# The last normalization moved to VectorE, its logits made row by row; one-hot matrices ahead of the expert tables; slot weights in two halves

## The chip, the cores and the metric

The kernel runs on one core of a Trainium2 chip. The metric is the device time of one execution in microseconds. A core has TensorE (PE: matrix products and transposes, results in PSUM), VectorE (DVE), ScalarE (ACT), GpSimd (POOL) and SyncE (SP, here the queue that issues most DMAs). Each engine runs its own list of instructions in order; they meet through semaphores, which an instruction raises when it ends and on which another waits.

## What is computed

Two blocks over x (4 batches of 512 rows of 512 values) and a context (4, 512, 256). First a selective state-space block, gated by the normalized x, then a mixture of eight experts in which each row goes to two.

```
x = x + ssm(ctx, z=layernorm(x))          # in_proj, causal conv of 4, silu, x_proj, dt_proj, softplus,
                                          # state = state*exp(d*A) + d*u*B ; y = state.C ; y = (y + D*u)*silu(z)
h = layernorm(x)                          # per row of 512 values, eps 1e-5
logits = h @ gate                         # (rows, 8)
w, idx = top_k(logits, 2); w = softmax(w)
x = x + sum_k w_k * (silu(h @ w0[idx_k]) * (h @ w1[idx_k])) @ wo[idx_k]
```

All matrices are fp32. In the experts each operand is split into two parts (hi and lo) and a product is made of three matmuls.

## The kernel before

**State-space block** (`mamba_block`). Work goes by units: batch (4), half of the channels (2), state (16), so 128 units. In a unit ScalarE makes dA, POOL the input term, VectorE two scans and most of the products with C, POOL the rest; TensorE broadcasts C into the PSUM bank `Cb` (line 663) and adds the unit's transposed states into `yT` (line 682). At the end of a half VectorE gates: g = yT * zsT (`drain_y`, line 572), and POOL adds g to xall (`add_y`, line 298). After a batch's second half come its statistics (`stats_2`, lines 584 and 588, VectorE), a first value of 1/sqrt(var + eps) as exp(-0.5 ln) (`guess_2`, lines 418 to 422, ScalarE), one Newton step and the negated mean (`rstd`, lines 236 to 246, POOL), the normalized rows xlnb (`xln`, line 439, ScalarE, one activation per tile of 128 rows), their transposes (`gate_T`, line 730, TensorE, with copies by ScalarE at line 339), the logits (`logits_of`, line 740, TensorE, all four tiles at once, after the last copies) and their copy (line 577, VectorE). SP stores xlnb and xall (`store_xln`, lines 200 and 201). For batches 0 to 2 all this is woven into the next batch's units; for the last it stands alone at the end. The transposes and logits share two PSUM banks, `pp`, whose uses are numbered in the list `USES`. All engines meet at the end of the block, and SP first waits there for both stores (line 224).

**Expert block** (`ffn_block`). SP loads the first expert's weights in six chunks of 1 MB (line 963). VectorE finds each row's two experts and weights (lines 1180 to 1204); two small matmuls (lines 1399 and 1400) count rows ahead; VectorE turns the counts into a slot for each row (lines 1211 to 1245): `quo` is the slot's tile of 128, `rem` its place there. Then, in this order:
- the tables of experts per tile (lines 1249 to 1275), ending in `tables_ok`, on which SP (line 966, a second load of the first chunks that is made only if the first expert is not number 0, then the next expert's loads, line 976) and ScalarE (the splits `w_hi`, line 1104) wait
- the one-hot matrices: S (line 1279, from quo), S times the row number (line 1284), R (line 1288, from rem, one half per choice k)
- TensorE: 32 matmuls of R and S_tok give the row number of each slot (line 1406)
- VectorE: the split `w_lo` of chunk 0 (line 1294), the token table (lines 1299 to 1305), the split of chunk 1, the weights times S (lines 1360 to 1365), which end in `RS_ok`
- POOL: the index (line 1034) and the gather of 128 rows of xln_dram (line 1040)
- TensorE: `x_T(0, 0)`, four transposes of the gathered rows (line 1415), 32 matmuls of R and S_w that give each slot's weight (line 1470), then `inner(0)`: four products of 12 matmuls (lines 1421 to 1423), each for one chunk. It waits for `xT_lo` (line 1318), and each product for its chunk's `w_lo`.

The loop over tiles follows, with weights changed when the expert does. The slot weights are read (`wtab`, lines 1374 and 1376) after the first tile's step.

## Time and profile before

| | us |
|---|---|
| median of 3 runs | 1330.68 |
| lowest and highest | 1323.72, 1347.05 |
| the profiled execution, its time | 1325.02 |
| its span | 1322.3 |
| mean granted clock of TensorE, as a share of full speed | 0.867 |

Busy share of the span by the profile: TensorE 85%, VectorE 57%, POOL 48%, ScalarE 40%. The profile's times count from the start of its span; the execution's own time is 2.7 us above the span. In the profile PE is TensorE's matmuls, PEld its weight loads, which overlap them. A row of the timeline has start, duration, engine, line, operation, output and inputs with shapes, the number of like instructions merged into it, and in brackets how long the engine had been idle before it and what released it. An fp32 matmul of the state-space block is recorded as two, an fp32 transpose as one.

### The profile page before, as it was taken

How to read it: one execution, taken by the hardware profiler on the slowest of the kernel's cores; microseconds unless marked ns; L12 is line 12 of the kernel's file. 1: busy time of each engine (PE TensorE's matmuls, PEld its weight loads, DVE VectorE, ACT ScalarE, POOL GpSimd, SP SyncE). 2: the span in 40 equal slices, each digit the busy share in tenths (PEclk: the TensorE clock that was granted, in tenths of full speed). 3: DMA queues.
4: the chain of work that ended last, by engine and by line, in shares of the span. 5: the costliest groups of instructions: out<-in, count | busy, mean ns of one | idle time of the engine just before them, and what ended most of it. 6: DMA issues, size and time to landing. Idle time of an engine off the chain costs nothing.

```text
span 1322.3 us, 19385 instructions
## 1 busy us (share of the span) xinstructions
PE 1124.1 (85%) x4940; PEld 837.2 (63%) x4940; DVE 751.0 (57%) x815; ACT 526.0 (40%) x707; POOL 639.7 (48%) x472
## 2 busy tenths in 40 slices
PE   4667988788868877833999999999999999999994
PEld 2234555446444645533788888888888888888883
DVE  3789899887998699837324353442532534324321
ACT  3775655674667464322213232321321323213210
POOL 0399899898989799613023222321222322213221
PEclk8587777686878577855999999999999999999998
DMA  5333232522242224045314243242421524314310
GB/s 180 123 102 103 67 119 88 167 78 91 75 158 82 88 75 156 1 145 204 137 48 167 97 152 125 87 154 76 171 96 48 174 104 160 104 46 174 103 40 25
DMA packets 65445, 145.08 MB, mean 110 GB/s; under 512 B 8655, under 2 KB 11215, under 8 KB 65409
## 3 DMA queue, kind: packets, MB, share of 16 engines
q1 hardware_dynamic: 56368, 116.34, 25.9%
q0 software_dynamic: 9040, 28.32, 6.5%
q8 instruction: 16, 0.26, 0.1%
q14 instruction: 21, 0.16, 0.0%
HBM read 320.53 MB, written 18.35 MB: 256 GB/s over the span
## 4 chain that ended last, share of the span: by engine, by line
PE 52%; DVE 2%; DMA 1%; issue 0%; POOL 0%; ACT 0%; POOLq 0%; DVEq 0%
PE hp L1423 11%; PE hp L1422 10%; PE hp L1421 10%; PE yp L1421 5%; PE yp L1423 5%; PE yp L1422 5%; PE tp L1462 2%; PE xp L1415 1%; PE hp L1406 1%; PE yp L1470 1%; DMA work<-xln_dram,index 0%; DMA work<-out_dram,acc_index 0%; DMA out_dram<-work,out_index 0%; DVE R L1288 0%; POOL index L1034 0%
## 5 line engine op out<-in xcount | busy, mean ns | idle before, releaser
L266 POOL TENSOR_TENSOR ring<-du,bB 128x1024 f32<-128x1024 f32 x128 | 299.3, 2357 | 75.5 <-DVE du L610 52.4
L539 DVE TENSOR_TENSOR_SCAN ring<-dA,ring 128x512 f32<-128x512 f32 x256 | 295.7, 1202 | 17.7 <-ACT dA L349 11.1
L349 ACT ACTIVATE dA<-delta,Acol 128x512 f32<-128x512 f32 x256 | 172.3, 687 | 170.4 <-DVE ring L539 168.0
L1421 PE MATMUL hp<-w_hi,xT_hi 128*128 128x512 f32 x592 | 236.4, 399 | 0.9 <-DVE xT_lo L1318 0.9
L1423 PE MATMUL hp<-w_hi,xT_lo 128*128 128x512 f32 x592 | 236.3, 399 | 0.0
L1422 PE MATMUL hp<-w_lo,xT_hi 128*128 128x512 f32 x592 | 234.1, 395 | 0.0
L682 PEld LDWEIGHTS yT<-ident,ring 128*128 128x128 f32 x1024 | 146.7, 172 | 97.3 <-issue 76.9
L663 PE MATMUL Cb<-xdbl,ident 48*128 48x512 f32 x176 | 126.9, 808 | 87.9 <-DVE ring L545 87.8
L682 PE MATMUL yT<-ident,ring 128*128 128x128 f32 x1024 | 172.9, 332 | 10.7 <-POOL ring L275 10.7
L1339 DVE TENSOR_TENSOR work<-hp,work 128x512 f32<-128x512 f32 x74 | 51.1, 690 | 229.3 <-PE hp L1423 226.2
L1058 POOL COPY out_index<-out_tab 128x1 uint32 x37 | 6.7, 181 | 355.0 <-DVE work L1325 355.0
L1294 DVE TENSOR_TENSOR w_lo<-stage,w_hi 128x2048 fp32r<-128x2048 f32 x48 | 109.1, 2288 | 36.0 <-ACT w_hi L1104 36.0
L1422 PEld LDWEIGHTS hp<-w_lo,xT_hi 128*128 128x128 f32 x592 | 111.6, 189 | 27.0
L1421 PEld LDWEIGHTS hp<-w_hi,xT_hi 128*128 128x128 f32 x592 | 111.8, 189 | 26.3 <-issue 1.1
L1423 PEld LDWEIGHTS hp<-w_hi,xT_lo 128*128 128x128 f32 x592 | 111.4, 188 | 26.1
L1421 PE MATMUL yp<-w_hi,iT_hi 128*128 128x512 f32 x296 | 121.2, 409 | 2.1 <-DVE iT_lo L1350 2.1
L545 DVE TENSOR_TENSOR ring<-Cb,ring 128x1024 f32<-128x1024 f32 x88 | 106.2, 1207 | 25.5 <-PE Cb L663 25.0
L1143 ACT CAST iT_hi<-tp 128x512 fp32r<-128x512 f32 x74 | 39.8, 590 | 194.8 <-PE tp L1462 194.8
L1423 PE MATMUL yp<-w_hi,iT_lo 128*128 128x512 f32 x296 | 116.7, 394 | 0.0
L1422 PE MATMUL yp<-w_lo,iT_hi 128*128 128x512 f32 x296 | 116.2, 393 | 0.0
L1325 DVE SCALAR_TENSOR_TENSOR work<-yp,wtab,work 128x512 f32<-128x512 f32 x37 | 27.8, 751 | 144.1 <-PE yp L1423 137.1
L663 PEld LDWEIGHTS Cb<-xdbl,ident 48*128 48x128 f32 x176 | 32.4, 229 | 119.4 <-DVE ring L545 60.7
(180 smaller groups left out, 1408.6 us busy)
## 6 DMA issues: line engine op xcount, KB each, us to landing
stage<-in_L_ffn_w_kernel_dram SPq DMA_DIRECT2D x160, 1024.0 KB
stage<-in_L_ffn_wo_kernel_dram SPq DMA_DIRECT2D x78, 1024.0 KB
bB<-bcs SPq DMA_DIRECT2D x64, 512.0 KB, 3.6
bC<-bcs SPq DMA_DIRECT2D x40, 256.0 KB, 4.4
xall<-in_x_dram SPq DMA_DIRECT2D x1, 4096.0 KB, 14.8
xln_dram<-xlnb SPq DMA_DIRECT2D x4, 1024.0 KB, 6.9
out_dram<-xall SPq DMA_DIRECT2D x4, 1024.0 KB, 9.1
ctx_rows<-in_ctx_dram SPq DMA_DIRECT2D x4, 512.0 KB, 5.5
```

Source lines behind the costliest of these rows:

```text
L266: g_.tensor_tensor(ring[:, q % RING, :].rearrange("p (e l) -> p e l", e=2), dub(b, h * 2 * L, 2 * L).rearrange("p (e l) -> p e l", e=2), B ...
L349: a_.activation(dA[r % SB][:, :], db(b, eb * L, L), ACT.Exp, scale=Acol[:, eb, n:n + 1]).then_inc(exp_done, 1)
L539: v_.tensor_tensor_scan(o, dA[r % SB][:, :], o, 0.0, ALU.mult, ALU.add).then_inc(scan_done, 1)
L545: v_.tensor_tensor(states, Cb[:, :].unsqueeze(1).to_broadcast([P, 2, L]), states, ALU.mult).then_inc(hc_dve, 1)
L663: t_.matmul(Cb[:, :], ident[0:rows, at:at + 1].to_broadcast([rows, P]), xdbl[:, b % 2, :], start=True, stop=True).then_inc(C_full, 1)
L682: last = t_.matmul(yT[:, t, e * P:(e + 1) * P], ring[:, q % RING, e * L + t * P:e * L + (t + 1) * P], ident[:, :], start=False, stop=(n == ...
L1143: s_.copy(iT_hi[:, 4 * h:4 * h + 4, :], tp[h][:, :].rearrange("p (k t) -> p k t", t=P)).then_inc(i_hi, 1)
L1294: v.tensor_tensor(w_lo[c][:, :, :], stage[c][:, :, :], w_hi[c][:, :, :].bitcast(fp32), ALU.subtract).then_inc(lo_done, 1)
L1339: v.tensor_tensor(inter[:, h, :], hp[2 + h][:, :], gated[:, h, :], ALU.mult).then_inc(inter_done, 1)
L1421: t_.matmul(bank[:, :], a_hi[:, k, :], b_hi[:, b, :], start=(start and k == ks[0]), stop=False)
L1422: t_.matmul(bank[:, :], a_hi[:, k, :], b_lo[:, b, :], start=False, stop=False)
L1423: last = t_.matmul(bank[:, :], a_lo[:, k, :], b_hi[:, b, :], start=False, stop=(stop and k == ks[-1]))
```

## The change

- The last batch's add of g (`add_y` on POOL) becomes a VectorE operation. POOL's `add_y` and `rstd_2` for the last batch go.
- The last batch's first value: VectorE adds eps (`var_last`), ScalarE, told ahead to load a named set of activation tables, does Ln and Exp.
- The Newton step and the negated mean: four VectorE operations in place of six of POOL.
- The copies of transposed tiles 1 and 3 go to VectorE; ScalarE keeps 0 and 2. TensorE makes the logits of a tile (`logits_row`) as soon as the next tile's transposes are issued, in `Cb` and not in a bank of `pp`; before that it waits for all of VectorE's products with C.
- In the routing the one-hot matrices S, S_tok and R come before the expert tables. Both follow on `routed` 31.
- The splits of chunks 0 and 1 on VectorE come after the weights times S.
- The 32 slot-weight matmuls are cut in two: the first sixteen before `x_T(0, 0)`, the others after `inner(0)`. `x_T(0, 0)` itself so comes after a wait for `RS_ok`.

```diff
--- before.py
+++ after.py
@@ -95,6 +95,8 @@
         consts_ok, stats1, rstd1_guess, rstd1_ok = sem("consts_ok"), sem("stats1"), sem("rstd1_guess"), sem("rstd1_ok")
         tap_done, u_ready, bcs_out = sem("tap_done"), sem("u_ready"), sem("bcs_out")
         x1_out = sem("x1_out")
+        logits_out = sem("logits_out")
+        var_last, last_step, logits_last = sem("var_last"), sem("last_step"), sem("logits_last")
         conv_step = [sem(f"conv_step{i}") for i in range(2)]
         abs_done, relu_done, soft_y, soft_w, soft_ln, soft_loss, soft_sub, delta_ready, du_ready, zs_ready = (
             sem(n) for n in ("abs_done", "relu_done", "soft_y", "soft_w", "soft_ln", "soft_loss", "soft_sub",
@@ -117,7 +119,7 @@
             USES += [f"{n}.{b - 1}" for n in ("G0", "G1") if rest]
             USES += [f"{n}.{b + 1}" for n in ("XP", "DT0", "DT1", "DT2", "DT3") if nxt]
             USES += [f"{n}.{b - 1}" for n in ("G2", "G3", "LG") if rest]
-        USES += [f"{n}.{NB - 1}" for n in ("G0", "G1", "G2", "G3", "LG")]
+        USES += [f"{n}.{NB - 1}" for n in ("G0", "G1", "G2", "G3")]
         USE = {n: i for i, n in enumerate(USES)}
 
         def bank(k):
@@ -326,8 +328,6 @@
                         add_ln(b + 1, 0)
                     if s == 31 and b + 1 < NB:
                         times_u(b + 1, 0)
-            add_y(NB - 1, 1)
-            rstd_2(NB - 1)
 
         @block.scalar
         def _(act):
@@ -521,9 +521,13 @@
                     if s == 31 and rest:
                         gate_T(b - 1, 2)
                         gate_T(b - 1, 3)
-            guess_2(NB - 1)
+            a_.preload_act_table_set("natural_log_exp_and_others")
+            act.wait_ge(var_last, 1)
+            a_.activation(rs2[:, 1, :], rs2[:, 0, :], ACT.Ln).then_inc(act_step, 1)
+            act.wait_ge(act_step, 2 * NB + 2)
+            a_.activation(rs2[:, 1, :], rs2[:, 1, :], ACT.Exp, scale=-0.5).then_inc(guess2, 1)
             xln(NB - 1)
-            for i in range(LB):
+            for i in (0, 2):
                 gate_T(NB - 1, i)
 
         @block.vector
@@ -638,8 +642,30 @@
                 times_c(NU - 1)
             logit_copy(NB - 2)
             drain_y(NB - 1, 1)
-            stats_2(NB - 1)
-            logit_copy(NB - 1)
+            b = NB - 1
+            xs = xall[:, b * LB:(b + 1) * LB, 2 * P:4 * P]
+            dve.wait_ge(y_gated, 2 * b + 2)
+            v_.tensor_tensor(xs, g[:, :, :], xs, ALU.add).then_inc(x_added, 1)
+            stats_2(b)
+            dve.wait_ge(stats2, NB)
+            v_.tensor_scalar(rs2[:, 0, :], mv2[:, :, 1], EPS, None, ALU.add).then_inc(var_last, 1)
+            dve.wait_ge(guess2, NB)
+            v_.tensor_tensor(rs2[:, 2, :], rs2[:, 0, :], rs2[:, 1, :], ALU.mult).then_inc(last_step, 1)
+            dve.wait_ge(last_step, 1)
+            v_.scalar_tensor_tensor(rs2[:, 2, :], rs2[:, 2, :], -0.5, rs2[:, 1, :], ALU.mult, ALU.mult).then_inc(last_step, 1)
+            dve.wait_ge(last_step, 2)
+            v_.scalar_tensor_tensor(rs2[:, 3, :], rs2[:, 2, :], 1.5, rs2[:, 1, :], ALU.add, ALU.mult).then_inc(last_step, 1)
+            dve.wait_ge(last_step, 3)
+            v_.scalar_tensor_tensor(nm2[:, :], mv2[:, :, 0], -1.0, rs2[:, 3, :], ALU.mult, ALU.mult).then_inc(rstd2_ok, 1)
+            for i in (1, 3):
+                k = USE[f"G{i}.{b}"]
+                if i == 1:
+                    j = USE[f"LG.{b - 1}"]
+                    dve.wait_ge(filled[j % 2], nth(j))
+                dve.wait_ge(filled[k % 2], nth(k))
+                v_.tensor_copy(gT[:, i, :], bank(k)[:, :]).then_inc(freed[k % 2], 1)
+            dve.wait_ge(logits_last, LB)
+            v_.tensor_copy(logits[:, b * LB:(b + 1) * LB, :].rearrange("p t e -> p (t e)"), Cb[:, 0:LB * 8]).then_inc(logits_out, 1)
 
         @block.tensor
         def _(pe):
@@ -739,6 +765,13 @@
                     for d in range(DI // P):
                         last = t_.matmul(o[:, i * 8:(i + 1) * 8], gT[:, i, d * P:(d + 1) * P], gate[:, d, :], start=(d == 0), stop=(d == DI // P - 1))
                 last.then_inc(done, 1)
+
+            def logits_row(i):
+                k = USE[f"G{i}.{NB - 1}"]
+                pe.wait_ge(freed[k % 2], nth(k))
+                for d in range(DI // P):
+                    last = t_.matmul(Cb[:, i * 8:(i + 1) * 8], gT[:, i, d * P:(d + 1) * P], gate[:, d, :], start=(d == 0), stop=(d == DI // P - 1))
+                last.then_inc(logits_last, 1)
 
             pe.wait_ge(ident_ok, 2)
             pe.wait_ge(small_in, 16 * 9)
@@ -802,9 +835,12 @@
                         logits_of(b - 1)
             for q in range(NU - LAG, NU):
                 acc(q)
+            pe.wait_ge(hc_dve, len(ON_DVE))
             for i in range(LB):
                 gate_T(NB - 1, i)
-            logits_of(NB - 1)
+                if i > 0:
+                    logits_row(i - 1)
+            logits_row(LB - 1)
 
 
 NE, FF, TOPK = 8, 1024, 2
@@ -920,6 +956,7 @@
         silu_done, x_hi, x_lo, i_hi, i_lo, inter_done, summed = (sem(n) for n in
             ("silu_done", "x_hi", "x_lo", "i_hi", "i_lo", "inter_done", "summed"))
         index_ok, acc_index_ok, out_index_ok = sem("index_ok"), sem("acc_index_ok"), sem("out_index_ok")
+        hot = sem("hot")
         xg_in = [sem(f"xg_in{i}") for i in range(2)]
         acc_in, scattered = sem("acc_in"), sem("scattered")
 
@@ -1244,6 +1281,18 @@
             v.tensor_copy(quo[:, :], quo_i[:, :]).then_inc(routed, 1)
             v.tensor_copy(rem[:, :], rem_i[:, :]).then_inc(routed, 1)
             dve.wait_ge(routed, 31)
+
+            v.tensor_tensor(S_lo, quo[:, :].unsqueeze(2).to_broadcast([P, TOPK * NT, ST]),
+                            io_st[:, :].unsqueeze(1).to_broadcast([P, TOPK * NT, ST]), ALU.is_equal).then_inc(hot, 1)
+            dve.wait_ge(hot, 1)
+            for k in range(TOPK):
+                part = slice(k * NT, (k + 1) * NT)
+                v.tensor_tensor(S_tok[:, part, :], S_lo[:, part, :].bitcast(fp32), tokid[:, :].unsqueeze(2).to_broadcast([P, NT, ST]), ALU.mult).then_inc(hot, 1)
+
+            dve.wait_ge(hot, 3)
+            for k in range(TOPK):
+                v.tensor_tensor(R[k][:, :, :], rem[:, k * NT:(k + 1) * NT].unsqueeze(2).to_broadcast([P, NT, P]),
+                                io128[:, :].unsqueeze(1).to_broadcast([P, NT, P]), ALU.is_equal).then_inc(RS_ok, 1)
 
             tend_b = over_t(tend[:, :], ST)
             v.tensor_tensor(table8[:, :, :], tend_b, over_e(io_st[:, :], ST), ALU.is_le).then_inc(routed, 1)
@@ -1276,32 +1325,18 @@
             dve.wait_ge(routed, 47)
             dve.sem_inc(tables_ok, 1)
 
-            v.tensor_tensor(S_lo, quo[:, :].unsqueeze(2).to_broadcast([P, TOPK * NT, ST]),
-                            io_st[:, :].unsqueeze(1).to_broadcast([P, TOPK * NT, ST]), ALU.is_equal).then_inc(routed, 1)
-            dve.wait_ge(routed, 48)
-            for k in range(TOPK):
-                part = slice(k * NT, (k + 1) * NT)
-                v.tensor_tensor(S_tok[:, part, :], S_lo[:, part, :].bitcast(fp32), tokid[:, :].unsqueeze(2).to_broadcast([P, NT, ST]), ALU.mult).then_inc(routed, 1)
-
-            dve.wait_ge(routed, 50)
-            for k in range(TOPK):
-                v.tensor_tensor(R[k][:, :, :], rem[:, k * NT:(k + 1) * NT].unsqueeze(2).to_broadcast([P, NT, P]),
-                                io128[:, :].unsqueeze(1).to_broadcast([P, NT, P]), ALU.is_equal).then_inc(RS_ok, 1)
-
             def split(c, done):
 
                 hold(dve, hi_done, done)
                 v.tensor_tensor(w_lo[c][:, :, :], stage[c][:, :, :], w_hi[c][:, :, :].bitcast(fp32), ALU.subtract).then_inc(lo_done, 1)
 
-            split(0, 1)
-
             dve.wait_ge(counted, 2 + TOPK)
             v.tensor_scalar(tok1[:, :], hp[2][:, 0:ST], -1.0, None, ALU.add).then_inc(routed, 1)
-            dve.wait_ge(routed, 51)
+            dve.wait_ge(routed, 48)
 
             v.tensor_scalar(tok_tab[:, :], tok1[:, :], 0.0, None, ALU.max).then_inc(routed, 1)
             v.tensor_scalar(none[:, :], tok1[:, :], 0.0, float(2 * TOK), ALU.is_lt, ALU.mult).then_inc(routed, 1)
-            dve.wait_ge(routed, 53)
+            dve.wait_ge(routed, 50)
             v.tensor_tensor(out_tab[:, :], tok1[:, :], none[:, :], ALU.add).then_inc(tabled, 1)
 
             def split_if(f, s, c):
@@ -1352,30 +1387,30 @@
                 for c in range(4, NC):
                     split_if(f, s, c)
 
-            split(1, 2)
-
             def over_s(a):
                 return a.rearrange("p k t -> p (k t)").unsqueeze(2).to_broadcast([P, TOPK * NT, ST])
 
             v.tensor_copy(wgt_hi[:, :, :], wgt[:, :, :]).then_inc(routed, 1)
-            dve.wait_ge(routed, 54)
+            dve.wait_ge(routed, 51)
             v.tensor_tensor(wgt_lo[:, :, :], wgt[:, :, :], wgt_hi[:, :, :].bitcast(fp32), ALU.subtract).then_inc(routed, 1)
             v.tensor_tensor(S_hi, S_lo.bitcast(fp32), over_s(wgt_hi[:, :, :].bitcast(fp32)), ALU.mult).then_inc(routed, 1)
-            dve.wait_ge(routed, 56)
+            dve.wait_ge(routed, 53)
             v.tensor_tensor(S_lo, S_lo.bitcast(fp32), over_s(wgt_lo[:, :, :]), ALU.mult).then_inc(routed, 1)
-            dve.wait_ge(routed, 57)
+            dve.wait_ge(routed, 54)
             dve.sem_inc(RS_ok, 1)
+            split(0, 1)
+            split(1, 2)
             x_part(0)
             split(2, 3)
             split(3, 4)
             step(0, 0, y=False)
 
-            dve.wait_ge(counted, 3 + TOPK)
+            dve.wait_ge(counted, 4 + TOPK)
             v.tensor_copy(wtab[:, :], yp[:, 0:ST]).then_inc(routed, 1)
-            dve.wait_ge(routed, 58)
+            dve.wait_ge(routed, 55)
             v.tensor_tensor(wtab[:, :], wtab[:, :], yp[:, ST:2 * ST], ALU.add).then_inc(routed, 1)
 
-            dve.wait_ge(routed, 59)
+            dve.wait_ge(routed, 56)
             dve.sem_inc(summed, 1)
             tiles = dve.value_load(tiles_i[0:1, 0:1], min_val=MIN_TILES, max_val=SLOT_TILES)
             with dve.Fori(0, TURNS) as t:
@@ -1462,14 +1497,16 @@
                         last = t_.transpose(tp[h][:, k * P:(k + 1) * P], inter[:, h, k * P:(k + 1) * P], identf[:, :])
                     last.then_inc(iT_done, 1)
 
-            x_T(0, 0)
-
-            pe.wait_ge(RS_ok, TOPK + 1)
-            for k in range(TOPK):
+            def slot_weights(k):
                 for t in range(NT):
                     last = t_.matmul(yp[:, 0:2 * ST], R[k][:, t, :], S_w[:, k * NT + t, :], start=(k + t == 0), stop=(k * NT + t == TOPK * NT - 1))
-            last.then_inc(counted, 1)
+                last.then_inc(counted, 1)
+
+            pe.wait_ge(RS_ok, TOPK + 1)
+            slot_weights(0)
+            x_T(0, 0)
             inner(0)
+            slot_weights(1)
             x_T(0, 1)
             inter_T(0)
```

## Rows read from the trace of the kernel before

**Rows 1.** Windows: busy us (instructions) by engine, granted clock, DMA share, GB/s.

```profile
0.00:560.97 560.97, 424.52 (x1712) 265.37 (x1712) 463.01 (x470) 323.20 (x458) 461.42 (x227) 0.76 0.32 103
562.19:586.60 24.41, 10.88 (x48) 10.04 (x48) 3.05 (x10) 8.35 (x13) 3.72 (x9) 0.50 0.24 87
586.60:630.84 44.24, 15.81 (x73) 15.43 (x73) 34.18 (x67) 9.38 (x7) 11.93 (x20) 0.50 0.64 222
630.84:633.54 2.70, 2.70 (x7) 2.12 (x8) 0.00 (x0) 0.00 (x0) 0.00 (x0) 0.50 1.06 405
643.23:1322.30 679.07, 660.50 (x3062) 536.45 (x3060) 248.84 (x267) 183.83 (x227) 162.60 (x217) 0.99 0.31 108
```

**Rows 2.** Timeline from the last gating to the last copy of logits.

```profile
560.97 1.22 DVE L572 TENSOR_TENSOR g<-yT,zsT 128x1024 f32<-128x1024 f32 x1 [2.65 <-PE yT L682]
562.27 2.34 POOL L298 TENSOR_TENSOR xall<-g,xall 128x1024 f32<-128x1024 f32 x1 [9.73 <-DVE g L572]
...
567.15 0.38 DVE L588 BATCH_NORM_AGGREGATE mv<-st 128x2 f32<-128x6 f32 x4
567.57 0.30 ACT L418 ACTIVATE rs<-mv,epsc 128x4 f32<-128x4 f32 x1 [16.86 <-DVE mv L588]
567.88 1.28 ACT L420 ACT_TABLE_LOAD   x1
...
570.97 0.20 POOL L236 TENSOR_TENSOR rs<-rs 128x4 f32<-128x4 f32 x1 [6.36 <-ACT rs L422]
...
572.64 2.93 ACT L439 ACTIVATE xlnb<-xall,nm,rs 128x512 f32<-128x512 f32 x4 [1.74 <-POOL nm L246]
...
573.50 1.97 PE L730 MATMUL pp<-ident,xlnb 128*128 128x128 f32 x8 [12.57 <-ACT xlnb L439]
575.47 1.05 ACT L339 ACTIVATE gT<-pp 128x512 f32<-128x512 f32 x2
...
578.92 6.97 PE L740 MATMUL pp<-gate,gT 128*128 128x8 f32 x32 [0.79 <-ACT gT L339]
585.93 0.19 DVE L577 COPY logits<-pp 128x32 f32<-128x32 f32 x1 [18.40 <-PE pp L740]
```

**Rows 3.** Waits of SP's queue from 560 to 660 us: in total, times, longest.

```profile
SPq L224 <- DMA out_dram<-xall: 6.6, 1, 6.6
...
SPq L35 <- PEq L35: 3.0, 1, 3.0
```

**Rows 4.** VectorE's add of two SBUF tiles of 128x1024, line 604.

```profile
L604 DVE TENSOR_TENSOR delta<-delta,du x1: 1226/1226/1226, 50.0 to 50.0; 128x1024 f32<-128x1024 f32 x1
```

**Rows 5.** Timeline of the routing, from the expert tables to the first tile.

```profile
596.69 0.51 DVE L1249 TENSOR_TENSOR work<-tend,io_st 128x336 f32<-128x336 f32 x1
...
601.79 1.56 DVE L1279 TENSOR_TENSOR S_w<-work,io_st 128x1344 fp32r<-128x1344 f32 x1
...
602.99 7.30 ACT L1104 CAST w_hi<-stage 128x2048 fp32r<-128x2048 f32 x4 [12.35 <-DMA stage<-in_L_ffn_w_kernel_dram]
...
605.04 4.50 DVE L1288 TENSOR_TENSOR R<-work 128x2048 fp32r<-128x2048 f32 x2
...
607.39 7.01 PE L1406 MATMUL hp<-S_tok,R 128*128 128x42 f32 x32 [15.45 <-DVE R L1288]
...
615.25 2.18 POOL L1034 COPY index<-tok_tab 128x1 uint32<-128x1 uint32 x1 [26.86 <-DVE out_tab L1305]
...
619.21 1.56 DVE L1365 TENSOR_TENSOR S_w<-S_w,wgt_lo 128x1344 fp32r<-128x1344 f32 x1
...
623.24 1.12 PE L1415 MATMUL xp<-identf,work 128*128 128x128 f32 x4 [8.84 <-DMA work<-xln_dram,index]
...
624.01 7.04 PE L1470 MATMUL yp<-S_w,R 128*128 128x84 f32 x32
...
625.01 0.69 DVE L1318 TENSOR_TENSOR xT_lo<-xp,xT_hi 128x512 fp32r<-128x512 f32 x1 [4.24 <-ACT xT_hi L1117]
...
625.62 4.48 DVE L1294 TENSOR_TENSOR w_lo<-stage,w_hi 128x2048 fp32r<-128x2048 f32 x2
```

## The prediction

> **What bounds the kernel now.** I read the stretches first: engine busy time and granted clock before the tail of the scans, in the tail, in the routing, and in the expert loop [rows 1]. In the first 561 us VectorE is busy 463 us; the diff leaves those instructions alone. From 643.23 us to the end TensorE is busy 660.5 of 679.1 us at a granted clock of 0.99; the loop is TensorE's, and the diff leaves it alone too. Between them lie 68.7 us (562.19 to 630.84) in which TensorE is busy 26.7 us and no engine is near full except VectorE in the routing (34.2 of 44.2 us). That is a chain of dependent steps, and everything the diff edits is in it. So the question is how much earlier line 1421's first matmul starts, and what is added behind it.
>
> I then read that chain in the order of time. In the tail [rows 2] the reader sees one engine at a time: VectorE's g, POOL's add (2.34 us), statistics, ScalarE's three small activations with two table loads, six POOL operations on 128x4 tiles, four ScalarE activations (2.93 us), transposes and copies, 16 fp32 products recorded as 32 matmuls (6.97 us), one copy. The DMA queue's own waits [rows 3] tell what else could end this stage: SP waits for the store of xall, then 3.0 us more for the engines. The last engine ends at 586.1, so the store had landed at about 583.1 and is 3 us from mattering. In the routing [rows 5] the tables stand ahead of the one-hot matrices, and the token table, the gather, the transposes and the 32 slot-weight matmuls (7.04 us) follow one another.
>
> **The tail.** Times are those of the trace before.
> - The add. POOL takes 2.34 us and starts 0.08 us after g ends at 562.19 [rows 2]. On VectorE a 128x1024 fp32 tensor_tensor took 1.23 us [rows 4], and it follows g on the same engine. Saved: 2.42 - 1.27 = 1.15 us.
> - The guess. From the end of the statistics at 567.53 to POOL's first operation at 570.97 pass 3.44 us [rows 2]: one activation of 0.30, two loads of 1.28, two activations of 0.20, gaps. After: one VectorE operation (0.17, as the routing's small ones [rows 5]), two activations of 0.20, three handoffs of about 0.04: 0.69 us. The load is issued while ScalarE sits idle (16.86 us before this point [rows 2]), so it costs nothing; without that cover it costs 1.28. Saved: 2.75 us.
> - The correction. Six POOL operations run from 570.97 to 572.64, 1.67 us [rows 2]. Four on VectorE at 0.17 + 0.04, and a handoff: 0.89. Saved: 0.78 us. The last activations so start at 572.64 - 1.15 - 2.75 - 0.78 = 567.96.
> - Logits. Before, 13.29 us pass from that start to the last copy at 585.93 [rows 2]. After: 2.93 for the activations and about 0.5 for ScalarE's copy of tile 0, which is queued behind them; then TensorE has the two remaining groups of four transposes (1.97 for two such groups) and the four rows (6.97): 3.4 + 8.94 = 12.3 us. VectorE's copies of tiles 1 and 3 lie beside a row of 1.74 us; a VectorE copy from PSUM is not shown, but g, twice its size, took 1.22 at most (562.19 - 560.97). Bounds: if rows and copies interleave badly nothing is saved here; if TensorE need not wait for ScalarE's copy, 1.9. I take 0.94. The new wait on hc_dve is for VectorE products that ended before 560 and costs nothing.
> Sum: 1.15 + 2.75 + 0.78 + 0.94 = 5.6 us; logits are copied at 580.3.
>
> The store is issued when the four activations end. Before, that was 575.57, so it took 7.5 us to land at 583.1 [rows 3]. After: 570.9 + 7.5 = 578.4, still 1.9 us ahead of the logits. The first load of weights, queued on SP behind it, moves up with them.
>
> In these rows a load is followed by its activation after 1.29 us, so a switch costs 1.3 us here [rows 2]. The Trainium skill (ScalarE: Activation LUTs, What ACT_TABLE_LOAD costs) adds a drain of about 1.38 us to each; by that the two loads would have taken 5.3 us. The row decides, since the whole stage took 3.44.
>
> **The routing**, still in the clock of before; the 5.6 us come on top.
> - The one-hot matrices move from 601.79 to 596.69, 5.10 us earlier [rows 5]. R's two halves (4.50 us from 605.04) end at 602.2 and 604.4. TensorE's 32 matmuls of line 1406, started at 607.39 and 7.01 us long, start at 602.3 and end at 609.3; the second sixteen need R's second half at 604.4, before the first sixteen end at 605.8.
> - The tables (from 596.69 to the start of the one-hot matrices, 5.10 us with the semaphore step) now run beside them, 604.4 to 609.5. They end 0.2 us after the matmuls: the two chains meet. POOL's first copy starts 0.85 us after the matmuls (614.40 to 615.25), so at 610.35 and not at 615.25: 4.9 us saved, 0.2 less than the move.
> - tables_ok comes at 609.5, not at 601.8. Behind it wait SP (the skipped second load, then the next expert's loads) and ScalarE's first splits. ScalarE started 1.35 us after the tables and took 7.30 for four [rows 5]: now 610.8 to 618.1. Its four ran without a pause from 602.99, so their data had landed by then or soon after, and nothing else holds them. The next expert's loads start at about 616.5 instead of 612; the reference gives 4096 rows to eight experts, so on average four tiles of 128 rows or more to each, at least 32 in the 679 us (18 to 21 us each), and the first change of weights is some 70 us away: covered.
> - The gather. From POOL's first copy (2.18 us) to the first transposes pass 623.24 - 615.25 = 7.99 us [rows 5]. The transposes start at 618.35; to the end of xT_lo pass 625.70 - 623.24 = 2.46, so 620.8.
> - The slot matrices follow the token table on VectorE, from 610.3: two products of 1.56 and two small operations of about 0.17, 3.5 us with the gaps, so they are ready at 613.9. Sixteen matmuls at 7.04 / 32 = 0.22 us end at 617.4, 0.95 us before the gathered rows are there: hidden. The splits of chunks 0 and 1 (2.24 each [rows 5]) end at 618.6 and are hidden as well; chunks 2 and 3 end at 625.4, while inner(0) wants them at 627 or later.
> - inner(0) starts at 620.85, not at 630.84: 10.0 us earlier. Behind it come the other sixteen matmuls. At the full clock they take half of 0.22 each, an estimate of 1.8 us (3.5 at the low one). All that follows is TensorE's chain: net 8.2 us.
> - The clock. It was granted at 0.50 (1.2 GHz) for all of the tail and routing and for 2.70 us of inner(0), whether TensorE worked or not [rows 1]; then it rose to 2.4 GHz. I take the same 2.7 us. The other bound is the whole time that TensorE had been at work before the rise, 10.3 us from 623.24: 7.6 more at half speed, a loss of 3.8 us. I take the first, since the 7.01 busy microseconds from 607.39 were followed by no rise.
>
> **Sum.** 5.6 + 8.2 = 13.8 us. The profiled execution has a span of 1322.3 and took 1325.0 us; it would take 1311.2, span 1308.5. The median of the runs shown is 1330.7, 5.7 above it: 1316.9. Three runs spread over 23 us, so I state 1315, between them and nearer the median.
>
> **Rivals.**
> - A: the clock stays low for 10 us of inner(0), as bounded above. Gain 10, time 1319. For: TensorE now has a gap of about 1.7 us just before inner(0), where before it had none. Against: the clock had not risen in 7.6 us of unbroken work ahead of inner(0), so that work is not shown to have helped.
> - B: two chains meet worse than drawn, or one table load stays. The token table, the slot matrices and ScalarE's splits each arrive within 1.5 us of what they must not pass (0.2, 0.95, 1.3). If all routing but the 4.9 us is lost, the gain is 10.5 at most; if the tail's loads also stay (2.6) it is 8: 1321. No row shows Ln and Exp without a load between; the Trainium skill (ScalarE: Activation LUTs, Table sets: the hidden batching unit) says that the named set holds both.
> - C: slower than before. One mechanism: the low clock lasts into the loop. Each microsecond of it costs half of one, so it decides when the low stretch is 28 us longer than before; at 45 us longer the loss is 22.5 and the time 1337, above the median of before. Against: 0.99 over the whole loop [rows 1].
> - D: gather and clock both come early (the gather with fewer loads beside it, the first copy of 2.18 us at a tenth of it): gain 17, 1312.
>
> **Chances.** Forecast (gain 11 to 17) 0.62; A 0.15; B 0.13; C 0.04; D 0.06. Gains of 8 to 17 around a median that itself moves some 8 us give 1305 to 1329. The forecast's own range is 1308 to 1322. A measurement of this kernel tells about 2% (27 us) from no change; only D with a lucky draw, or a disturbed median, reaches it: faster 0.05, same 0.93, slower 0.02.
>
> **What would show it.** One table load ahead of the last statistics, none between Ln and Exp; the last activations starting 4.7 us earlier; the store landing before the logits copy; POOL's first copy some 10.5 us earlier than 615.25; 8 us from there to line 1415; line 1470 in two blocks, 3.5 us before inner(0) and 1.8 after; the low clock ending 2.7 us into inner(0); the loop's 679 us unchanged. The prediction is wrong if the store or tables_ok ends last in its stage, if the low clock outlasts chunk 0, or if the loop's length moves by more than 2 us.

## The result, and the profile after

| | before | after |
|---|---|---|
| median of 3 runs, us | 1330.68 | 1311.01 |
| lowest and highest | 1323.72, 1347.05 | 1310.08, 1316.20 |
| the profiled execution's span | 1322.3 | 1309.3 |

The ratio of after to before is 0.9895 (95% interval 0.9864 to 0.9926): 1.05% faster, some 14 us, clear of the noise and within 2%. With eleven runs of before and five of after on another occasion it was 0.9883 (0.9831 to 0.9934). Ratios here leave out the executions that lie over 1.5% above the fastest of their kernel, among them that of 1347.05 us above and one of 3601.26 us of the changed kernel on the other occasion.

The span fell by 13.0 us. The windows of after, with the columns of [rows 1], show where:

```profile
0.00:562.91 562.91, 424.80 (x1712) 265.11 (x1712) 463.06 (x470) 324.48 (x459) 461.35 (x227) 0.77 0.31 103
564.13:582.49 18.36, 10.44 (x48) 9.97 (x48) 6.48 (x19) 4.42 (x8) 0.18 (x2) 0.50 0.31 115
582.49:615.53 33.04, 12.76 (x57) 11.98 (x57) 29.84 (x66) 8.72 (x7) 10.23 (x18) 0.50 0.62 219
615.53:618.40 2.87, 2.87 (x7) 2.29 (x8) 2.87 (x2) 0.68 (x1) 2.60 (x2) 0.50 1.05 401
```

The tail, from the end of g to the first reduction of logits, is 18.4 us instead of 24.4; the routing, to the first matmul of inner(0), 33.0 instead of 44.2. TensorE's work in the two is nearly the same; POOL's in the tail went from 3.72 us to 0.18, VectorE's from 3.05 to 6.48. The clock is low in both, as before. The scans, whose code is the same, ended 1.9 us later in this execution, and the stretch after inner(1) took 677.1 us against 676.4.

The tail of after (timeline, columns as in [rows 2]):

```profile
552.67 1.28 ACT L524 ACT_TABLE_LOAD   x1
...
562.91 1.22 DVE L576 TENSOR_TENSOR g<-yT,zsT 128x1024 f32<-128x1024 f32 x1 [2.64 <-PE yT L708]
564.17 1.23 DVE L648 TENSOR_TENSOR xall<-g,xall 128x1024 f32<-128x1024 f32 x1
...
568.55 0.20 ACT L526 ACTIVATE rs<-rs 128x4 f32<-128x4 f32 x1 [14.60 <-DVE rs L651]
568.79 0.21 ACT L528 ACTIVATE rs<-rs 128x4 f32<-128x4 f32 x1
569.03 0.17 DVE L653 TENSOR_TENSOR rs<-rs 128x4 f32<-128x4 f32 x1 [0.51 <-ACT rs L528]
...
569.82 2.93 ACT L439 ACTIVATE xlnb<-xall,nm,rs 128x512 f32<-128x512 f32 x4 [0.82 <-DVE nm L659]
...
573.28 1.88 PE L773 MATMUL Cb<-gate,gT 128*128 128x8 f32 x8 [0.61 <-ACT gT L339]
...
581.81 0.19 DVE L668 COPY logits<-Cb 128x32 f32<-128x32 f32 x1 [2.52 <-PE Cb L773]
```

The one table load begins 15.9 us ahead of Ln, and none stands between Ln and Exp. The waits of SP's queue say that the store still lands first, now 2.1 us ahead of the engines and not 3.0 [rows 3]:

```profile
SPq L226 <- DMA out_dram<-xall: 6.1, 1, 6.1
SPq L35 <- PEq L35: 2.1, 1, 2.1
```

The routing of after, to be read against [rows 5]:

```profile
595.83 4.49 DVE L1294 TENSOR_TENSOR R<-work 128x2048 fp32r<-128x2048 f32 x2
598.17 7.02 PE L1441 MATMUL hp<-S_tok,R 128*128 128x42 f32 x32 [10.36 <-DVE R L1294]
...
606.15 0.19 POOL L1071 COPY index<-tok_tab 128x1 uint32<-128x1 uint32 x1 [21.88 <-DVE out_tab L1340]
...
606.53 7.31 ACT L1141 CAST w_hi<-stage 128x2048 fp32r<-128x2048 f32 x4 [20.01 <-DMA stage<-in_L_ffn_w_kernel_dram]
606.63 2.33 POOL L1077 DMA_INDIRECT work<-xln_dram,index  x1 [0.29 <-POOL index L1071]
...
609.58 3.64 PE L1502 MATMUL yp<-S_w,R 128*128 128x84 f32 x16 [4.38 <-DVEq L1400]
609.61 4.50 DVE L1331 TENSOR_TENSOR w_lo<-stage,w_hi 128x2048 fp32r<-128x2048 f32 x2
...
613.01 1.11 PE L1450 MATMUL xp<-identf,work 128*128 128x128 f32 x4
614.16 0.59 ACT L1154 CAST xT_hi<-xp 128x512 fp32r<-128x512 f32 x1 [0.32 <-PE xp L1450]
614.78 0.69 DVE L1353 TENSOR_TENSOR xT_lo<-xp,xT_hi 128x512 fp32r<-128x512 f32 x1 [0.67 <-ACT xT_hi L1154]
```

Two things differ from the forecast. POOL's first copy takes 0.19 us instead of 2.18. And the transposes of line 1450 no longer wait for the gathered rows: those landed 4.7 us after the gather's issue, at 611.3, but TensorE comes to them at 613.0, right behind the sixteen slot-weight matmuls. ScalarE's four splits end at 613.84 and VectorE's two at 614.11, just ahead of the steps that follow them there. Three chains arrive within 1.1 us.

### The profile page after: what moved, and what is told of

Its sections match the earlier page's. It is cut to its first block, busy times and chain, and to the rows that moved or that the text cites. A ratio compares the mean times of both kernels' runs of the same rounds, so it can differ in the third digit from the quotient of the medians.

```text
span 1309.3 us, 19380 instructions
## 1 busy us (share of the span) xinstructions
PE 1124.2 (86%) x4940; PEld 836.9 (64%) x4940; DVE 754.4 (58%) x823; ACT 523.3 (40%) x703; POOL 639.2 (49%) x465
## 3 DMA queue, kind: packets, MB, share of 16 engines
HBM read 320.53 MB, written 18.35 MB: 259 GB/s over the span
## 4 chain that ended last, share of the span: by engine, by line
PE 52%; DVE 2%; issue 0%; ACT 0%; POOL 0%; ACTq 0%; DVEq 0%; POOLq 0%
PE hp L1458 11%; PE hp L1457 11%; PE hp L1456 11%; PE yp L1456 5%; PE yp L1458 5%; PE yp L1457 5%; PE tp L1497 2%; PE xp L1450 1%; PE yp L1502 0%; DVE R L1294 0%; DVE S_tok L1290 0%; DVE S_w L1285 0%; DVE S_w L1398 0%; DVE S_w L1396 0%; DVE xT_lo L1353 0%
## 5 line engine op out<-in xcount | busy, mean ns | idle before, releaser
L543 DVE TENSOR_TENSOR_SCAN ring<-dA,ring 128x512 f32<-128x512 f32 x256 | 295.9, 1204 | 17.7 <-ACT dA L349 11.0
L1456 PEld LDWEIGHTS hp<-w_hi,xT_hi 128*128 128x128 f32 x592 | 111.8, 189 | 27.8 <-DVE xT_lo L1353 1.8
L1360 DVE SCALAR_TENSOR_TENSOR work<-yp,wtab,work 128x512 f32<-128x512 f32 x37 | 27.8, 750 | 145.0 <-PE yp L1458 145.0
## 6 DMA issues: line engine op xcount, KB each, us to landing
xall<-in_x_dram SPq DMA_DIRECT2D x1, 4096.0 KB, 15.1
```

What stands on the lines that cost most here:

```text
L543: v_.tensor_tensor_scan(o, dA[r % SB][:, :], o, 0.0, ALU.mult, ALU.add).then_inc(scan_done, 1)
L1456: t_.matmul(bank[:, :], a_hi[:, k, :], b_hi[:, b, :], start=(start and k == ks[0]), stop=False)
```

## The experiments

All stages below come from one profile of each kernel, so that the noise of the scans stays out. Times are us from the end of g to the first reduction of logits ("tail"), from there to POOL's first copy, to the first transposes, to inner(0), and to the first matmul of inner(1); "sum" is from g to inner(1). After inner(1) all kernels took 675.7 to 677.2. The first four columns repeat to 0.02 us in the two profiles of the changed kernel (after, changed_again), but the last two differ by 0.9: from the start of inner(0) the clock stayed at 1.2 GHz for 2.9 us in the one and for some 5 in the other. In the other kernels without added matmuls that stretch was between some 2 us (onehot_first) and some 5.5 (split1_late, other_order). So a difference in "sum" of 1 us or less between two kernels is not shown; the columns up to inner(0) are the firmer measure.

| kernel | tail | copy | transposes | inner(0) | inner(1) | sum |
|---|---|---|---|---|---|---|
| before | 24.41 | 28.65 | 36.64 | 44.24 | 59.34 | 83.75 |
| after | 18.36 | 23.66 | 30.52 | 33.04 | 49.70 | 68.06 |
| tail_only | 18.33 | 28.66 | 36.77 | 44.37 | 60.62 | 78.95 |
| routing_only | 24.39 | 23.65 | 30.51 | 33.02 | 49.98 | 74.37 |
| onehot_first | 24.43 | 29.00 | 37.03 | 44.63 | 59.52 | 83.95 |
| halves_only | 24.41 | 28.66 | 37.72 | 40.24 | 57.21 | 81.62 |
| split1_late | 24.40 | 28.65 | 33.91 | 41.51 | 57.85 | 82.25 |
| no_table_set | 19.61 | 23.66 | 30.52 | 33.03 | 50.64 | 70.25 |
| slots_after | 18.34 | 23.65 | 28.79 | 32.59 | 51.22 | 69.56 |
| changed_again | 18.34 | 23.66 | 30.53 | 33.04 | 50.64 | 68.98 |
| warm_fill | 17.56 | 23.65 | 29.18 | 32.59 | 49.38 | 66.94 |
| other_order | 18.35 | 23.65 | 27.79 | 30.31 | 48.99 | 67.34 |
| order_and_fill | 17.46 | 23.65 | 27.87 | 29.93 | 47.55 | 65.01 |
| best | 16.38 | 23.68 | 28.92 | 30.92 | 47.00 | 63.38 |

**The two halves of the change.** tail_only has the new `mamba_block` and the old `ffn_block`, routing_only the reverse.

> Only the last normalization and its logits are changed; the routing is that of before. My theory (the two parts add): the last copy of logits comes 6 us earlier after the end of g than before (17.7 us against 23.7), everything from there on is unchanged (44.2 us to the first matmul of inner(0), about 679 us after it), so 6 us or 0.45% in all. Rival (the store takes over): the copy is early but SP waits for the store, and the routing starts less than 5 us earlier.

Measured: ratio 0.9964 (0.9933 to 0.9995); the first reduction 6.1 us sooner, as expected.

> Only the routing is changed; the tail is that of before. Theory: from the first reduction of logits to inner(0) 33.0 us instead of 44.2, and 1.9 us more for the second half of the slot weights: 9.3 us or 0.7% in all. With the tail alone this sums to what both give together. Rival (the parts lean on each other): less than 7 us, as the 6 MB of first weights now land no earlier while their reader comes earlier.

Measured: ratio 0.9945 (0.9919 to 0.9971); inner(0) 11.2 us sooner, inner(1) 9.4. The tail's 6.1 and the routing's 11.2 up to inner(0) are those of the whole change to within 0.03 us: the two add, and neither takes from the other. What does not add neatly is the length of inner(0) itself. From its start to inner(1) tail_only took 16.3 us where before took 15.1, with the same instructions: its clock was still low after 5 us of inner(0), in before it rose within 3.

**Parts of the routing.** onehot_first moves only the one-hot block of before ahead of the tables:

```diff
             dve.wait_ge(routed, 31)
+            v.tensor_tensor(S_lo, quo[:, :].unsqueeze(2).to_broadcast([P, TOPK * NT, ST]),
...
             tend_b = over_t(tend[:, :], ST)
...
             dve.sem_inc(tables_ok, 1)
-            v.tensor_tensor(S_lo, quo[:, :].unsqueeze(2).to_broadcast([P, TOPK * NT, ST]),
...
```

> The kernel before with one part of the change: the one-hot matrices ahead of the expert tables, all else as before, so the split of chunk 0 still stands ahead of the token table on VectorE. Theory (this part is worth nothing without the move of the split): the tables end 22.9 us after the first reduction, ScalarE's first split at 26.0, VectorE's split of chunk 0 at 28.3, so POOL's first copy starts at 29.1 instead of 28.7 and inner(0) at 44.7 instead of 44.2. Rival (the part carries its 4.9 us by itself): POOL's first copy at 23.7.

Measured: the first copy at 29.0 and inner(0) at 44.6, as the theory had it. The rows show why (timeline of onehot_first):

```profile
609.62 7.30 ACT L1105 CAST w_hi<-stage 128x2048 fp32r<-128x2048 f32 x4 [20.01 <-DMA stage<-in_L_ffn_w_kernel_dram]
611.55 2.29 DVE L1295 TENSOR_TENSOR w_lo<-stage,w_hi 128x2048 fp32r<-128x2048 f32 x1 [3.28 <-ACT w_hi L1105]
614.42 2.29 DVE L1295 TENSOR_TENSOR w_lo<-stage,w_hi 128x2048 fp32r<-128x2048 f32 x1
614.57 2.19 POOL L1035 COPY index<-tok_tab 128x1 uint32<-128x1 uint32 x1 [27.21 <-DVE out_tab L1306]
```

VectorE sits idle for 3.28 us ahead of the split of chunk 0, since ScalarE's part waits for tables_ok, and the token table is queued behind it. The reordering alone costs 0.4 us up to inner(0). Its 4.9 us come only with the move of the splits: routing_only, with the splits moved as well, has the copy at 23.65, and the halves, its other difference, leave the copy where it was (halves_only, 28.66).

halves_only cuts the slot weights in two and changes nothing else:

```diff
-            x_T(0, 0)
-
             pe.wait_ge(RS_ok, TOPK + 1)
-            for k in range(TOPK):
...
+            slot_weights(0)
+            x_T(0, 0)
             inner(0)
+            slot_weights(1)
```

> The kernel before with one part of the change: the slot weights in two halves around the first transposes and inner(0). Theory: the transposes now wait for the weights times S, which are ready 34.2 us after the first reduction, and for sixteen matmuls: they start at 37.9 instead of 36.6, inner(0) at 40.3 instead of 44.2, and 1.9 us come behind it: 2.0 us in all. Rival (the half stays in the way as much as the whole): inner(0) after 43.

Measured: transposes at 37.7, inner(0) at 40.2, sum 2.1 us shorter; expected 37.9, 40.3 and 2.0.

**POOL's slow first copy.** split1_late is the kernel before with one line moved:

```diff
-            split(1, 2)
-
             def over_s(a):
...
             dve.sem_inc(RS_ok, 1)
+            split(1, 2)
             x_part(0)
```

> The kernel before with one step moved: the split of chunk 1 on VectorE, which started just before POOL's first copy of the index, now follows the weights times S. Theory (the copy of 2.18 us was held up by VectorE's 128x2048 operation with two operands in SBUF): the copy takes 0.2 us, the gathered rows are there about 1 to 2 us earlier and inner(0) starts as much earlier. Rival (the first copy is slow because it is the first use of the line or of the table): it still takes 2.2 us and nothing moves.

Measured: the copy takes 0.19 us, and the transposes and inner(0) come 2.7 us sooner: 2.0 by the copy, the other 0.7 between the gather's issue and the transposes (4.8 us from 615.17 instead of 5.5 from 617.73), and why is not shown. The sum is 1.5 us shorter only, since the clock rose late here. Timeline of split1_late:

```profile
614.68 0.19 POOL L1034 COPY index<-tok_tab 128x1 uint32<-128x1 uint32 x1 [26.86 <-DVE out_tab L1305]
...
614.85 1.55 DVE L1361 TENSOR_TENSOR S_w<-S_w,wgt_hi 128x1344 fp32r<-128x1344 f32 x1
615.17 2.32 POOL L1040 DMA_INDIRECT work<-xln_dram,index  x1 [0.30 <-POOL index L1034]
...
619.94 1.11 PE L1414 MATMUL xp<-identf,work 128*128 128x128 f32 x4 [6.11 <-DMA work<-xln_dram,index]
```

In the kernel before, the copy began at 615.25 [rows 5], 0.14 us behind the start of a split that ran from 615.11 to 617.39, and ended at 617.43. In onehot_first above the split ends at 616.71 and the copy at 616.76. So the copy stands still until VectorE's operation ends. The rival, a first use of the line, falls: the first use takes 0.19 us when VectorE does something short. The Trainium skill (GPSIMD Engine Reference, Specifications) says that POOL shares its SBUF interfaces with VectorE, with contention from VectorE instructions that have two inputs in SBUF; the split is one, and the trace agrees. Whether it is the two inputs or only the length of the operation no run separates. In the change this gain came as a side effect that the prediction had not counted: the splits moved, and the first copy no longer met one.

**The table load.** no_table_set is the changed kernel without one line:

```diff
-            a_.preload_act_table_set("natural_log_exp_and_others")
```

> The changed kernel without the line that loads the named set of tables ahead of time. Theory: two loads of 1.28 us return, one ahead of Ln and one ahead of Exp, and the last activations start 2.6 us later after g than in the changed kernel (8.3 against 5.7 us); the store still lands first, so the whole is 2.6 us longer. Rival (the load was hidden in any case): one load returns at most and under 1.5 us.

Measured: the rival. One load returns, and the tail is 1.25 us longer, not 2.6. Timeline of no_table_set:

```profile
541.31 1.28 ACT L525 ACT_TABLE_LOAD   x1
...
563.71 0.20 ACT L525 ACTIVATE rs<-rs 128x4 f32<-128x4 f32 x1 [21.11 <-DVE rs L650]
563.93 1.28 ACT L527 ACT_TABLE_LOAD   x1
565.23 0.20 ACT L527 ACTIVATE rs<-rs 128x4 f32<-128x4 f32 x1
```

The load for Ln goes out 22 us ahead, since in the changed program it stands ahead of the wait for `var_last`. In the kernel before it stood behind ScalarE's own addition of eps, hence behind the wait for the statistics [rows 2]. So of the 2.6 us of loads that left the path, one half leaves when the addition goes to VectorE, without a named set, and the naming adds the other. What the naming alone would do, with the addition left on ScalarE, no run shows.

**Which chain starts inner(0).** slots_after puts all slot weights behind inner(0):

```diff
-            pe.wait_ge(RS_ok, TOPK + 1)
-            slot_weights(0)
             x_T(0, 0)
             inner(0)
+            pe.wait_ge(RS_ok, TOPK + 1)
+            slot_weights(0)
             slot_weights(1)
```

> The changed kernel with all 32 slot-weight matmuls after inner(0). In the changed kernel the transposes of the gathered rows start 30.5 us after the first reduction of logits, right behind the first sixteen slot-weight matmuls, while the rows landed at about 28.8. Theory (three chains meet within half a microsecond: these matmuls, ScalarE's four splits, VectorE's two): the transposes start at 28.9, but inner(0) only at 32.7 instead of 33.0, and behind it 3.7 us of slot weights instead of 1.9, so 1.4 us longer in all. Rival (the matmuls alone set the start): inner(0) at 31.4 and the whole no longer than now.

Measured: transposes at 28.8, so in the changed kernel the rows had been there 1.7 us before TensorE came to them; inner(0) at 32.6, only 0.45 sooner. The sum is 1.5 us longer than in the first profile of after and 0.6 than in the second; behind inner(0) the slot weights took 3.5 us instead of 1.7, which less the 0.45 is 1.3 us. Timeline of slots_after:

```profile
607.75 1.12 PE L1450 MATMUL xp<-identf,work 128*128 128x128 f32 x4 [6.09 <-DMA work<-xln_dram,index]
...
610.20 0.57 ACT L1154 CAST xT_hi<-xp 128x512 fp32r<-128x512 f32 x1
```

The transposes end at 608.9, but ScalarE converts them only at 610.2, behind its fourth split. The halves of the slot weights are well placed in the order that the change chose.

other_order changes that order: ScalarE takes the first rows after two splits and VectorE after one, the weights times S follow the four splits, and all slot weights follow `x_T(0, 1)`.

```diff
@@ ScalarE @@
-            for c in range(4):
+            for c in range(2):
                 split(c, 2)
             x_part(0)
+            for c in range(2, 4):
+                split(c, 2)
@@ VectorE @@
-            v.tensor_copy(wgt_hi[:, :, :], wgt[:, :, :]).then_inc(routed, 1)
...
-            dve.sem_inc(RS_ok, 1)
             split(0, 1)
-            split(1, 2)
             x_part(0)
+            split(1, 2)
             split(2, 3)
             split(3, 4)
+            v.tensor_copy(wgt_hi[:, :, :], wgt[:, :, :]).then_inc(routed, 1)
...
+            dve.sem_inc(RS_ok, 1)
@@ TensorE @@
             x_T(0, 0)
             inner(0)
             x_T(0, 1)
+            pe.wait_ge(RS_ok, TOPK + 1)
+            slot_weights(0)
+            slot_weights(1)
```

> The changed kernel with another order in the routing: transposes of the first rows and inner(0) before all slot weights, these after the second rows' transposes; ScalarE and VectorE split the first rows right after their first or second chunk; the weights times S after the four splits. Theory (POOL is held up by VectorE's wide operations, the three chains no longer meet): the first gather is issued in 1.0 us instead of 2.3, the transposes start at 27.5 us after the first reduction instead of 30.5, inner(0) at 30.0 instead of 33.0; behind it 1.2 us are given back by 32 instead of 16 slot-weight matmuls, partly beside a wait; 1.8 us in all. Rival (the gather's landing time does not follow the issue): inner(0) no earlier than 32.

Measured: ratio to before 0.9852 (0.9798 to 0.9907). Transposes at 27.8, inner(0) at 30.3, 2.7 us sooner than in the changed kernel; the sum is 0.7 and 1.6 us shorter than in its two profiles, 1.8 expected. Timeline of other_order, with nothing on VectorE between the token table and the split:

```profile
605.96 1.21 POOL L1077 DMA_INDIRECT work<-xln_dram,index  x1 [0.29 <-POOL index L1071]
...
607.80 2.29 DVE L1333 TENSOR_TENSOR w_lo<-stage,w_hi 128x2048 fp32r<-128x2048 f32 x1 [2.38 <-ACT w_hi L1141]
```

The first gather's issue takes 1.21 us, beside the weights times S it takes 2.33. It is the second sign of POOL's being held up. But an issue is not always held: the second gather's, begun at 607.66 and so 0.14 us ahead of a split, took 0.97 us beside it, while in after the second one, begun 0.18 us behind the start of a split, took 2.97.

**The clock.** warm_fill adds matmuls to the changed kernel whose product nobody reads; `warm(n)` issues n of 512 columns into `tp[0]`, ten after the counts and seven after the row numbers of the slots:

```diff
             pe.wait_ge(hc_dve, len(ON_DVE))
+            pe.wait_ge(scan_done, 2 * NU)
+            for _ in range(7):
+                t_.matmul(dA[0][:, :], ident[:, :], ub(NB - 1, 0, L), start=True, stop=True)
...
+            warm(10)
...
+            warm(7)
```

> The changed kernel with matmuls whose product nobody reads where TensorE is idle: seven fp32 ones of 512 columns after the last accumulation, ten after the counts, seven after the row numbers. Theory (the clock is at its low level in tail and routing because TensorE does little there, and it is what makes these matmuls slow): granted clock near 1.0 in part of both stages; the logits 4 us sooner after the last activations, but the first reduction only 2 us sooner, as the store of xall then ends last; first sixteen slot weights 1.8 instead of 3.6 us, inner(0) 0.3 us sooner and 1.4 us shorter; 3.7 us in all. Rival (the clock stays low whatever is issued, or the added matmuls get in the way): nothing is won, or the whole is longer.

Measured: ratio to before 0.9861 (0.9795 to 0.9926); sum 1.1 and 2.0 us shorter than in the two profiles of the changed kernel, not 3.7. The clock can be raised, but it did not stay. Windows of warm_fill (columns as in [rows 1]):

```profile
567.84:570.64 2.80, 2.80 (x7) 0.95 (x5) 2.15 (x11) 0.41 (x2) 0.00 (x0) 1.00 0.00 0
573.30:575.40 2.10, 0.95 (x8) 0.95 (x9) 0.69 (x1) 1.10 (x2) 0.00 (x0) 0.99 0.26 98
575.40:582.20 6.80, 6.76 (x33) 6.67 (x33) 0.69 (x1) 0.60 (x1) 0.00 (x0) 0.50 0.75 278
...
612.70:615.47 2.77, 0.02 (x1) 0.00 (x1) 2.53 (x3) 2.75 (x3) 2.49 (x3) 1.00 0.54 171
615.47:616.30 0.83, 0.83 (x4) 0.69 (x5) 0.83 (x1) 0.53 (x1) 0.82 (x2) 1.00 1.06 417
616.30:619.60 3.30, 3.30 (x9) 2.58 (x8) 3.30 (x2) 0.00 (x0) 3.03 (x2) 0.50 1.04 395
```

It was at 2.4 GHz when the transposes began and for the first row of logits, and back at 1.2 GHz for the other three. It was high when inner(0) started, fell after 0.8 us and stayed low for 3.3. Ahead of both falls TensorE had stood idle: 1.2 us twice in the tail, 2.7 us before inner(0).

order_and_fill joins the two edits.

> Both: the other order and the added matmuls. Theory: 2 us from the tail, 3.5 us up to inner(0), 1.4 us in it, 1.2 us given back: 5.7 us less than the changed kernel. Rival: the two gains exclude each other, since both act on the same stretch, and no more than the better one of them is left.

Measured: ratio 0.9823 (0.9755 to 0.9890); sum 65.0, 3.1 and 4.0 us less than in the two profiles of the changed kernel, where 5.7 were expected. It is 2.3 us less than other_order and 1.9 less than warm_fill, so the gains do not exclude each other, but the clock's share is small again.

**A version that beats both.** best is order_and_fill with three small steps:

```diff
@@ ScalarE's copies @@
-            for i in (0, 2):
+            for i in (1, 3):
@@ VectorE's copies @@
-            for i in (1, 3):
+            for i in (0, 2):
@@ TensorE @@
-            for _ in range(7):
+            for _ in range(8):
...
             x_T(0, 0)
+            warm(1)
             inner(0)
```

> The other order with the added matmuls, and three small steps: VectorE copies tiles 0 and 2 and ScalarE 1 and 3, one more added matmul in the tail, and one between the first transposes and inner(0). Theory: the first row of logits no longer waits for ScalarE's queue, so the first reduction comes 1.3 us earlier than in the changed kernel (0.8 from the clock, 0.5 from the copy); from the first reduction to inner(1) 47.5 us or less instead of 49.7; 3.5 us less than the changed kernel, ratio to the kernel before 0.986. Rival (what these stages win is lost in the noise of the scans): the medians of the two don't differ by more than 1 us, though the stages do.

> The changed kernel once more, beside the last version on the same chip. Stages as in its first profile: 18.4 us from the end of g to the first reduction, 33.0 to inner(0), 677 from inner(1) to the end; inner(0) between 12.4 and 13.7 us, by the moment at which the clock rises. Ratio to the kernel before 0.989.

Measured on one chip: best 0.9813 (0.9772 to 0.9854), median of six 1304.5; the changed kernel 0.9883 (0.9831 to 0.9934), median of five 1316.3. The medians of the two are 11.8 us apart and their profiled spans 11.3; of these 5.6 us are the stages (63.4 against 69.0) and 4.8 the end of the scans, whose code is the same. The two intervals overlap slightly, though five of best's six runs lie below the lowest of the changed kernel's, 1309.3. What the stages show is 5.6 us against this profile of the changed kernel and 4.7 against its first, where 3.5 were expected. Windows and SP's wait of best:

```profile
572.00:576.20 4.20, 4.13 (x37) 4.00 (x37) 0.72 (x2) 1.13 (x3) 0.00 (x0) 1.00 0.79 290
576.20:579.82 3.62, 0.00 (x0) 0.00 (x0) 0.16 (x1) 0.00 (x0) 0.17 (x2) 0.59 0.65 243
```

```profile
SPq L226 <- DMA out_dram<-xall: 6.1, 1, 6.1
...
SPq L35 <- PEq L35: 0.2, 1, 0.2
```

TensorE's idle gaps ahead of the transposes and of the first row shrank from 1.2 us each to 0.37 and 0.15: the eighth added matmul fills the one, and the first copy, on the engine that is free, shortens the other. The clock stayed at 2.4 GHz through all four rows, and the logits are copied 12.7 us after g instead of 17.7; which of the two steps kept the clock up no run separates. But the first reduction comes only 2.0 us sooner: TensorE stands still for 3.6 us, and the other engines for 3.3 behind the copy of the logits, until the store of xall has landed. Of the 5 us, 3 went to a new wait. The added matmuls also cost something: the transposes came 1.05 us later than in order_and_fill, since the last of the seven were still running. They had started later, because the 32 matmuls ahead of them took 5.8 us instead of 4.2: in best the clock fell to 1.2 GHz for the second sixteen, after an idle gap of 0.75 us ahead of the first.

## Why the prediction was right, point by point

- **What bounds the kernel.** Right: nothing outside the chain between g and inner(1) moved beyond the scatter of the same code.
- **The add, the guess, the correction.** From the end of g to the statistics 1.30 us instead of 2.46, saved 1.16 (1.15 stated); from their end at 568.31 to the next VectorE operation at 569.03, 0.72 instead of 3.44 (0.69); then 0.79 instead of 1.67 (0.89). The last activations start 4.76 us sooner after g; 4.68 stated. Right in sum, but no_table_set showed that the words around it were too simple: half of the loads' price goes with the addition of eps, without the named set.
- **Logits.** 11.99 us instead of 13.29: 1.30 saved, 0.94 stated. The term was set a little too small: from the first row's start at 573.28 the two groups of transposes and the four rows took 8.5 us, and not the 8.94 that the rows of before add up to; why is not shown. VectorE's copy of 128x512 from PSUM took 0.69 us.
- **The store.** Not last in its stage, 2.1 us to spare (1.9 stated). best shows that this reserve is real: with the store issued where it is, 2.0 us were all that a tail faster by 5 could win.
- **The token table.** POOL's first copy 4.99 us sooner after the first reduction (4.9). Tables and matmuls met, as stated: both end at 605.19.
- **The gather, the step that failed.** The 7.99 us "from POOL's first copy (2.18 us) to the first transposes" were carried over unchanged. They contained 2.0 us in which the copy stood still beside a split, and the change takes that split away: the copy took 0.19 us. Another 0.8 us fell away between the gather's issue and its landing (4.7 us instead of 5.5), and why stays open. So the rows landed 28.8 us after the first reduction and not 31.75. The prediction had the short copy only in rival D, as a chance.
- **The slot weights' cover.** "0.95 us before the gathered rows are there: hidden": their end was right (30.7 us after the first reduction, 30.8 stated), the cover was not. The rows came 2.9 us sooner than stated, so the matmuls were last, by 1.7 us, and took back part of it. slots_after shows that the next chain, ScalarE's splits, stood only 0.45 us behind.
- **inner(0).** 11.2 us sooner, 10.0 stated: the sum of the two points above. The second half of the slot weights took 1.7 us of TensorE (628.25 to 629.95; 1.8 stated).
- **The clock.** Low for 2.9 us of inner(0) (2.7 stated), so rival A did not come. But 2.7 was carried over from one execution, and that it came so near was luck: the time from inner(0) to inner(1) less the slot weights is 15.1 us in before, 16.3 in tail_only and split1_late, 15.0 and 15.9 in the two profiles of after.
- **The sum.** The stages gave 15.7 us in the first profile of after and 14.8 in the second; 13.8 stated. The span fell by 13.0, since the scans took 1.9 us more and the loop 0.7. The median fell by 19.7, the ratio of the runs says 14. That 14 lies so near 13.8 is in part luck: two steps were wrong in opposite directions, by 2.9 us for the rows' landing and 1.7 for the slot weights' cover, and the 1 to 2 us by which the stages gave more than stated are less than the scatter of the runs. Rivals B and C did not come: splits, slot matrices and token table all arrived in time. Of D the short copy came and the early clock did not.

## What to carry to other kernels

A stage that is one chain of small steps can be summed row by row to about a microsecond, but a duration may be carried over only with its neighbours: ask of each row that looks too long (2.18 us for a copy of one column) what ran beside it, and whether the change moves that. Reordering one queue pays only if the steps that now come too early for their inputs move as well; the three moves of the routing brought inner(0) forward by -0.4, 4.0 and 2.7 us alone (one-hot matrices, halves, a split), and by 11.2 together with the other split's move; the halves give 1.7 of it back behind inner(0). And when a chain is shortened, look for the next one: here three ended within 1.1 us of each other in one stage, and in the other a store stood 2 us behind.

## What the runs showed of the hardware

- POOL's small copy of one column took 0.19 us alone and 2.18 to 2.32 us beside a VectorE subtraction of two 128x2048 SBUF tiles that had started before it, ending 0.04 to 0.05 us after it. The issue of an indirect DMA took 0.97 us in the loop (median of 39 in after), 1.21 with VectorE idle beside it, 2.33 with VectorE's 1.55 us products of two SBUF tiles, and 2.97 behind the start of such a subtraction.
- Where a table load runs depends on what stands ahead of its function. In no_table_set, where Ln is the first activation behind the wait, the load ran at 541.31, 22 us before the wait ended; in before, where the addition of eps stands between the wait and Ln, it ran at 567.88, behind the addition.
- Matmuls of no use raised TensorE's clock in a stage where it had been at 1.2 GHz throughout. With gaps of 1.2 us between the bursts it fell back after the first row; in best, with gaps of 0.4 us and less, it held at 1.00 for all four. In best's routing it fell once more, after 0.75 us idle and sixteen matmuls of 42 columns.
- The scatter between executions of the same code is mostly made in the scans: g ended between 559.3 and 572.4 us over these profiles. In the latest of them, halves_only, VectorE waited longer for TensorE's broadcast than in the kernel before, 28.6 us against 25.0 by the releaser, at a granted clock of 0.74 against 0.77 from 60 to 560 us (groups of lines of before, then of halves_only, 0 to 560 us):

```profile
L545 DVE TENSOR_TENSOR ring<-Cb,ring 128x1024 f32<-128x1024 f32 x88 | 106.2, 1207 | 25.5 <-PE Cb L663 25.0
```

```profile
L545 DVE TENSOR_TENSOR ring<-Cb,ring 128x1024 f32<-128x1024 f32 x88 | 106.4, 1209 | 29.0 <-PE Cb L663 28.6
```

That is 3.6 of the 10.2 us; the rest of the scatter stays open.
